# Attention and routed experts on one core: reads by 64 tokens, another order of the loads and of the routing steps

## The reference

```python
q_prime = relu(q @ Wqf.T); k_prime = relu(k @ Wkf.T) * mask      # q, k, v: projections, per head
kv = k_prime.T @ v;  k_sum = sum(k_prime)
att = (q_prime @ kv) / (q_prime @ k_sum + 1e-8)
x = x + att @ Wo.T + bo
p = softmax(layernorm(x) @ gate_w);  w, e = top_2(p);  w = w / sum(w)
x = x + sum_k w_k * ((silu(xn @ w1[e_k]) * (xn @ w3[e_k])) @ w2[e_k])   # xn = layernorm(x)
```

## Time and profile before

| | us |
|---|---|
| median of three runs | 497.66 |
| lowest, highest | 497.05, 499.25 |
| the profiled execution's own time | 499.79 |
| its span, first to last instruction | 497.9 |
| first expert product | 163.34 |
| first product of tile 4 | 209.09 |
| last output | 481.51 |

### The profile page before, as it was taken

The page is one execution under the profiler, slowest core; times in us unless marked ns, Lnnn a source line. Parts: engine busy times, 40 slices in busy tenths (PEclk is TensorE's granted clock), DMA queues, the critical chain, the costliest instruction groups (busy, mean ns, idle before and its releaser), DMA issues.

```text
span 497.9 us, 11763 instructions
## 1 busy us (share of the span) xinstructions
PE 447.2 (90%) x3665; PEld 416.3 (84%) x3666; DVE 208.6 (42%) x569; ACT 228.1 (46%) x477; POOL 231.6 (47%) x222
## 2 busy tenths in 40 slices
PE   3873999999989899799898999999999999999960
PEld 3773999889978788699898999899999999999960
DVE  4413766785485666623232323143323232332310
ACT  3614776647756255235542364263355264323210
POOL 5302638575858436119681249158139348121211
PEclk9995999999989899889999999999999999999985
DMA  8461101137102823381736212713621212121210
GB/s 257 142 224 41 44 24 65 65 103 231 63 22 76 286 44 101 89 268 33 243 80 200 44 32 34 244 32 92 194 32 33 32 32 30 34 32 32 35 23 11
DMA packets 34519, 46.05 MB, mean 92 GB/s; under 512 B 3488, under 2 KB 29344, under 8 KB 34464
## 3 DMA queue, kind: packets, MB, share of 16 engines
q1 hardware_dynamic: 22304, 31.82, 19.1%
q0 software_dynamic: 6576, 8.82, 10.3%
q10 hardware_dynamic: 5584, 4.76, 3.6%
HBM read 32.63 MB, written 12.76 MB: 91 GB/s over the span
## 4 chain that ended last, share of the span: by engine, by line
PE 66%; DMA 10%; DVE 8%; issue 5%; POOL 4%; ACT 3%; POOLq 1%; ACTq 0%; SPq 0%; DVEq 0%
PE bank L803 26%; PE twin L821 14%; DMA out_rows<-qf,x_all 6%; PE twin L674 5%; PE bank L840 3%; POOL w_lo L489 3%; DVE prob L1208 3%; PE bank L591 3%; PE bank L545 2%; PE bank L572 2%; DMA raw<-in_ctxT 2%; PE twin L665 2%; PE bank L546 2%; PE bank L608 2%; PE bank L547 2%
## 5 line engine op out<-in xcount | busy, mean ns | idle before, releaser
L499 POOL DMA_INDIRECT out_rows<-qf,x_all x35 | 54.6, 1560 | 158.9 <-ACT qf L1033 156.6
L803 PE MATMUL bank<-w_hi,c_hi 128*128 (+1 forms) x280 | 107.6, 384 | 4.1 <-POOL w_lo L489 1.6
L803 PE MATMUL bank<-w_lo,c_hi 128*128 (+1 forms) x280 | 104.1, 372 | 0.0
L821 PE MATMUL twin<-w_hi,kv_halves 128*128 (+1 forms) x490 | 97.2, 290 | 5.5 <-issue 5.0
L1292 DVE TENSOR_TENSOR x_all<-bank,x_all 128x448 f32<-128x448 f32 x70 | 43.4, 623 | 112.8 <-ACT x_all L1050 112.7
L821 PEld LDWEIGHTS twin<-w_hi,kv_halves 128*128 128x128 f32 x490 | 79.2, 192 | 6.4 <-issue 6.4
L1050 ACT ACTIVATE x_all<-bank 128x448 f32<-128x448 f32 x70 | 37.8, 544 | 96.3 <-PE bank L803 90.8
L489 POOL TENSOR_TENSOR w_lo<-raw,w_hi x18 | 76.2, 4436 | 10.0 <-ACT w_hi L1043 7.5
L803 PE MATMUL bank<-w_hi,c_lo 128*128 (+1 forms) x280 | 80.6, 370 | 0.0
L1298 DVE TENSOR_TENSOR kv_halves<-bank,kv_halves 128x512 fp32r<-128x512 f32 x66 | 38.6, 624 | 80.9 <-ACT kv_halves L1055 80.7
L821 PE MATMUL twin<-w_lo,kv_halves 128*128 (+1 forms) x245 | 69.7, 285 | 0.0
(11 more groups left out here) (218 smaller groups left out, 730.8 us busy)
## 6 DMA issues: line engine op xcount, KB each, us to landing
raw<-in_w SPq DMA_DIRECT2D x24, 896.0 KB, 7.5
x_all<-bucket ACTq DMA_DIRECT2D x31, 129.0 KB, 2.1
raw<-in_ctxT SPq DMA_DIRECT2D x8, 256.0 KB, 3.2
out_rows<-x_all SPq DMA_DIRECT2D x8, 256.0 KB, 2.1
bucket<-pad_rows SPq DMA_DIRECT2D x13, 129.0 KB, 3.3
x_all<-in_x SPq DMA_DIRECT2D x2, 512.0 KB, 6.5
x_all<-bucket SPq DMA_DIRECT2D x6, 129.0 KB, 2.7
x_all<-in_x SPq DMA_DIRECT2D x1, 768.0 KB, 6.6
```

Of the source, the lines that this page charges most:

```text
L499: pool.indirect_dma_start(out=out, out_offset=bass.IndirectOffsetOnAxis(ap=x_in[:, v, D:D + 1].bitcast(U32), axis=0), in_=y[:, v, :], in_o ...
L803: last = nc.tensor.matmul(bank[b][:, 0:MC], stationary[:, k, :], w[:, bass.ds(at + (of + k * M + c * MC), MC)], start=(k == 0 and part == ...
L821: last = nc.tensor.matmul(bank[6][:, 0:D], stationary[:, k, :], w[:, bass.ds(at + (2 * W13 + k * D), D)], start=(k == 0 and part == 0 and ...
```

## The change

- TensorE's `read` handles 64 tokens at a time, on array columns 0 to 63 and 64 to 127 in turn.
- SyncE loads the contexts of pairs 2 and 3 ahead of expert 0, which it loads in pass 2 of its loop. Later it writes all eight pads first, loads tile 4 from a constant row, then tile 5.
- VectorE makes the low keys (in round 7: the residual of pair 6) ahead of `best_two`. `split_x(1)`, `choices` of the last pair, the first list steps and `split_x(4)` move up in the hand-written part.
- TensorE and ScalarE take the transposes of tiles 1 and 4 earlier. GpSimd starts the last scatter ahead of an add. The number of tiles is read before the loops, and the last output takes a constant place of its weights.

```diff
...
             sp.dma_start(bucket[PAD_AT:PAD_AT + P, :], pad_rows[:]).then_inc(pad_stored[1], 16)
-            sp.wait_ge(wk_halves, 2)
-            sp.wait_ge(bdk_halves, 2)
-            sp.wait_ge(wv_halves, 2)
-            sp.wait_ge(bdq_halves, 2)
-            sp.wait_ge(wo_halves, 2)
-            load_expert(0)
             for i in range(NPR):
+                if i == 2:
+                    sp.wait_ge(wk_halves, 2)
+                    sp.wait_ge(bdk_halves, 2)
+                    sp.wait_ge(wv_halves, 2)
+                    sp.wait_ge(bdq_halves, 2)
+                    sp.wait_ge(wo_halves, 2)
+                    load_expert(0)
                 if i >= 2:
...
                 sp.dma_start(bucket[bass.ds(n + e * CAP, P), :], pad_rows[:]).then_inc(pad_stored[min(e, 2)], 16)
-            def load_first(t):
-                at = sp.value_load(tab_row[0:1, t:t + 1], min_val=0, max_val=PAD_AT)
-                sp.wait_ge(y_added, 16 * (t - 3))
-                sp.dma_start(x_in[:, t % 4, :], bucket[bass.ds(at, P), :]).then_inc(x_in_loaded[t % 4], 16)
             sp.wait_ge(list_ready, 1)
-            pad(0)
-            pad(1)
+            for e in range(E):
+                pad(e)
             for odd in range(2):
                 sp.wait_ge(scattered[odd], 32 * NPR)
+            sp.wait_ge(pad_stored[0], 16)
+            sp.wait_ge(y_added, 16)
+            sp.dma_start(x_in[:, 0, :], bucket[2 * P:3 * P, :]).then_inc(x_in_loaded[0], 16)
+            sp.wait_ge(pad_stored[1], 16 * 2)
             sp.wait_ge(list_ready, 3)
-            sp.wait_ge(pad_stored[0], 16)
-            load_first(AHEAD)
-            for e in range(2, E):
-                pad(e)
-            sp.wait_ge(pad_stored[1], 16 * 2)
-            load_first(AHEAD + 1)
+            at = sp.value_load(tab_row[0:1, AHEAD + 1:AHEAD + 2], min_val=0, max_val=PAD_AT)
+            sp.wait_ge(y_added, 16 * 2)
+            sp.dma_start(x_in[:, 1, :], bucket[bass.ds(at, P), :]).then_inc(x_in_loaded[1], 16)
             sp.wait_ge(logits_done, NPR)
...
             scatter(NPR - 2)
+            scatter(NPR - 1)
             add(1, 1)
-            scatter(NPR - 1)
             add(2, 2)
...
                 for j in range(PAIRS):
-                    last = nc.tensor.matmul(bank[6 + o][:, j * 2 * AUG:(j + 1) * 2 * AUG], qf[:, j, o * P:(o + 1) * P],
-                                            kv[:, o, j, :], start=True, stop=True)
+                    for half in range(2):
+                        at = o * P + half * (P // 2)
+                        last = nc.tensor.matmul(bank[6 + o][half * (P // 2):(half + 1) * (P // 2), j * 2 * AUG:(j + 1) * 2 * AUG],
+                                                qf[:, j, at:at + P // 2], kv[:, o, j, :], start=True, stop=True)
                 if o == 1:
...
                 last.then_inc(h_done, 1)
-            def output(t):
-                _, at = slot_at(t)
+            def output(t, at=None):
+                if at is None:
+                    _, at = slot_at(t)
                 if tile_live(t, -1):
...
             read(NPR - 1, 1)
+            x_transposes(1, 1)
             hidden(0, 1)
             transpose_x2(NPR - 2)
-            x_transposes(1, 1)
             transpose_attention(NPR - 1)
...
             hidden(3, 1)
+            x_transposes(4, 0)
             g_transposes(3)
...
             pe.wait_ge(list_ready, 7)
-            x_transposes(4, 0)
+            n = tiles_used(pe)
             tiles_of_mixture(pe, mix)
-            output(tiles_used(pe) - 1)
+            output(n - 1, (E - 1) % 2 * WALL)
         @block.scalar
...
                 at = act.value_load(tab_row[0:1, bass.ds(t, 1)], min_val=0, max_val=PAD_AT)
+                if isinstance(t, int) and t == AHEAD + 2:
+                    act.wait_ge(pad_stored[2], 16 * (E - 2))
                 if tile_live(t, -4):
...
                 act.wait_ge(xT_done, t + 1)
+                if isinstance(t, int) and t == 1:
+                    act.wait_ge(h_done, 2)
                 nc.scalar.copy(x_hi.rearrange("p k n -> p (k n)"), rows_bank(t)[:, 0:D]).then_inc(x_hi_ready, 1)
...
             silus(0, 0)
+            evacuate_x(1)
             silus(0, 1)
...
             high_attention(NPR - 1)
-            evacuate_x(1)
             exponents(NPR - 2)
...
             silus(3, 1)
+            evacuate_x(4)
             high_g(3)
-            evacuate_x(4)
-            act.wait_ge(pad_stored[2], 16 * (E - 2))
             act.wait_ge(list_ready, 7)
...
                 low_attention(i - 1)
+                if i + 1 < NPR:
+                    low_channels(kT_lo, kT_hi, bank[4], bk_s, kT_ready, kT_lo_ready, i + 1)
+                else:
+                    residual(i - 1)
                 if i >= 2:
                     best_two(i - 2)
-                if i + 1 < NPR:
-                    low_channels(kT_lo, kT_hi, bank[4], bk_s, kT_ready, kT_lo_ready, i + 1)
-                if i >= 2:
                     choices(i - 2)
...
             split_x(0)
-            residual(NPR - 2)
             rank_slots(NPR - 3)
...
             attend(NPR - 1)
+            split_x(1)
             gates(0, 1)
             low_attention(NPR - 1)
-            split_x(1)
             maxima(NPR - 2)
...
             best_two(NPR - 1)
+            choices(NPR - 1)
             gates(2, 0)
-            choices(NPR - 1)
             dve.wait_ge(list_step, 1)
...
             nc.vector.tensor_copy(tab_count[:], n_row[:]).then_inc(list_ready, 1)
-            gates(2, 1)
-            split_x(3)
             link(nc.vector.tensor_tensor(more, n_row[:].rearrange("a (e o) -> a e o", o=1).to_broadcast([1, E, NT]),
...
             link(nc.vector.tensor_scalar(ends[:, 0, :], n_tiles[:], 1.0, None, ALU.max))
-            low_g(2)
             for i, by in enumerate((1, 2, 4)):
...
                 link(nc.vector.tensor_tensor(ends[:, i + 1, by:E], ends[:, i, by:E], ends[:, i, 0:E - by], ALU.add))
+            gates(2, 1)
+            split_x(3)
+            low_g(2)
             link(nc.vector.tensor_tensor(past, tile_no[:].rearrange("a (t o) -> a t o", o=1).to_broadcast([1, TILES, E]), wide(ends[:, 3, :]), ALU.is_ge))
...
             gates(3, 1)
+            split_x(4)
             link(nc.vector.memset(lists[:, 4, 0:AHEAD + 1], 0.0))
...
             low_g(3)
-            split_x(4)
             dve.wait_ge(list_ready, 7)
...
```

## The result

| | before | after |
|---|---|---|
| runs shown, us | 497.38 (497.05 to 499.25, 4 runs) | 481.63 (480.38 to 483.93, 4 runs) |
| profiled execution, us (span) | 499.79 (497.9) | 480.38 (478.6) |

The ratio is 0.9681, 95% interval 0.9632 to 0.973. The direction was forecast, the size was not: 473.3, with a range up to 480.5.

A forecast was written before the change was run, and what follows sets the result against it. TensorE, working in 447.2 of 497.9 us, was taken as the bound. Terms 12.1 + 5.8 + 3.7 + 1.2 + 1.6 = 24.4 off the profiled 499.79 give 475.4, or 473.3 for the median; range 467 to 480.5.

The forecast's parts named there:

- Part 1: Contexts loaded before expert 0: TensorE's 10.2 us wait and the slow clock after it go, 12.1 us net.
- rival of the moved wait: Expert 0's transfer ends at 45, not 40.5; ScalarE then TensorE stand 2.5 to 4 us in round 2: 477, chance 0.12.
- the attention, 0.7: Next wait in pair 1's round: VectorE needs 1.37 us to the scaled attention, TensorE has 0.91 of work; about 0.7 us.
- Part 2: Reads on 64 columns take 1.05 us instead of 1.81; 5.8 us saved where TensorE sets the pace.
- rivals of 1.8 and 3.6 us: Read times: halves' weight loads take turns, 1.8 (479, chance 0.12); each record costs as before, 3.6 (503, chance 0.03).
- reads gain nothing: The two halves' weight loads take turns, so a read stays at 1.8 us: 479, chance 0.12.
- Part 3: Low keys ahead of `best_two`: TensorE's waits for them go; 3.7 us in rounds 4 to 7, reads included.
- routing does not hold: `prob` slips in before GpSimd's pieces; rounds 4 to 7 run at 15.5, 9 us more gained: 464, chance 0.12.
- The residual: Residual of pair 6 ahead of `prob`: the first expert product no longer waits for it; saves 0.8 us.
- Part 4: Early expert tiles: tile 1's transposes and tile 4's load come earlier, net of new waits; 1.2 us.
- the 0.8 less at tile 4: First product of tile 4, hanging on the last list and two register loads, comes at 208.3, 0.8 us earlier.
- Part 5: Tail: two of five register loads in TensorE's 4.10 us idle before the last output go; 1.6 us.

The follow-up runs named there:

- e15: The changed kernel with all reads back on 128 columns, on the fourth chip: 486.55 us, 0.9731 of the kernel before.
- e18: The changed kernel itself, unaltered, run again on the fourth chip: 481.2 us, 0.9626 of the kernel before.
- e3_keys_late: The changed kernel with low keys and the residual of pair 6 behind `best_two` again: 484.83 us, 0.965 of the kernel before.
- e14_changed_third: The changed kernel itself, unaltered, profiled again on the third chip: 490.75 us, 0.9834 of the kernel before.
- e12_fill: The changed kernel with the four second transposes done twice, ahead of the query features: 489.3 us, 0.9806 of the kernel before.

## Why the prediction was right and wrong

**Part 1 (12.1) held.** The wait is gone, ScalarE took the context at 26.75, and expert 0 arrived in time, so the rival of the moved wait fell. Round 2's values came 13.0 us earlier; with the two reads of the round I had 13.6. The new wait was not the one I named (the attention, 0.7) but 0.95 us before the transposes of x, whose normalising GpSimd holds, and 0.47 before the query features.

**Part 2 (5.8): the record was right, its worth was not.** 32 records take 1.06 us, forecast 1.05, so the rivals of 1.8 and 3.6 us fell. By e15 and e18 the first rank is 1.55 us earlier with short reads at equal clock (60.38, 58.83), where I had 3.0 for rounds 1 and 2. Up to `rank(1)` I had 17.15 and got 14.5. The step that failed is that TensorE sets the pace of rounds 1, 2 and 3, so that each keeps all of its 1.5 us: rounds 1 and 2 now have the two waits of part 1, and 0.65 us before the second transposes for low halves of the queries behind a held normalising, and from `rank(0)` on the wait for the low context takes 0.68. From there to `rank(4)` short reads are worth nothing. The rival "reads gain nothing" had 479 and comes nearer to 481.63 than the forecast, but by luck: a read did fall to 1.06. The Trainium skill (TensorE: Matmul & The Clock Gate, "The mechanism") has a weight load overlap a matmul only if the row group differs; the trace disagrees, as it did for the gathers: 0.033 us a record.

**Part 3 (3.7) failed by its main term.** From `rank(1)` to `rank(3)` 0.1 us was saved, not 1.9; from `rank(3)` to `rank(5)` 0.7, not 1.0. I had routing hold one round in two, at 17.4 us, and TensorE the other at 15.5 and 0.6. That is the step that failed: the rounds last 17.6 to 18.3, and no round falls to TensorE's own 15.9. Over the four rounds to `rank(4)` e15 and e18 are equally long, though TensorE has 1.1 to 1.5 us more to do in each of e15's. I take it that a round behind a held one is held too, since its `slots`, low context and `chosen` all come from the same two engines. It was my rival "routing does not hold" turned round; I gave a chance to the side on which it holds less and none to that on which it holds more. The keys themselves were right: no wait for low keys is left, and e3_keys_late has 2.8 us of it again. The residual saved 0.7 for 0.8. `prob` outlasted more than one piece once more (3.80 us, from within the second to the end of the third): the trace still disagrees with the Trainium skill's SBUF, State Buffer, "SBUF: two separate sides", by which the port pair is held for one instruction.

**Part 4 (1.2) failed at tile 4.** The early tiles gave 1.15 us (41.0 to 39.86 from tile 0 to the end of tile 3's hidden product), which with the last read's 0.75 is what I had. But the 0.8 less at tile 4 became 1.25 more. A pad took 8.90 / 8 = 1.11 us and not 0.97, the load was out at 186.41, 0.9 us before the end of tile 3's product, and behind the 1.70 us wait come the split, the last list and the register loads, 2.94 us of issue where I had 1.2. With two pads 4.6 to 5.1 us are enough, as before the change (4.76).

**Part 5 (1.6) held:** TensorE idles 2.25 us and not 4.10, and the shorter idle kept the upper clock: the last output takes 2.7 us, not 4.86. That brought little, as ScalarE is in its own tests until 467.1 and evacuates then: last output to the end is 15.9 for 16.4.

**The sum.** 24.4 less 4.85 in the rounds, 2.0 at tile 4, and 1.8 more than forecast behind it (0.25 in the tail's idle, 1.0 in the expert tiles, 0.5 at the end) is 19.3, the profiled gain. The other 3.6 us up to the medians are how two executions lay in their spread; I had allowed for the 2.1 of the one before. I had treated that spread as noise around a fixed clock; the mean clock of the four executions after goes from 0.976 to 0.964.

## What to carry to other kernels

A wait that is removed from the busiest engine is only worth what the next loop leaves: work out the period of every loop through the other engines, and if one is longer than the shortened round, it paces all rounds, not every second one. Before making an instruction of the bound engine cheaper, look for the short two-input VectorE operation that stands beside GpSimd's long ones and is on the way to the busy engine's next input; taking it out, with two pads for eight, gave 7.9 us beside reads of 128 columns (486.55 to 478.63), where the new read gave 5.4 on the same chip. And measure a small gain on more than one chip, with both kernels in each comparison.

## What was unexpected of the hardware

- **The clock can fall behind small waits.** A round with a few idle stretches of 0.2 to 0.9 us can end in some 3 to 7 us at the lower level (1.2 GHz): in e14_changed_third 0.16 and 0.57 us idle at 120.8 and 122.2, then 0.50 at 123 to 125. The changed kernel's first result had 1.6 us idle a round in one or two pieces, and no fall until the last, while e15_reads_128_again, after 0.83 us idle before 130.18, ran its next 22.89 us at 0.68. The time goes with the mean: over the 22 executions of the changed kernel on record a straight line falls by 4.6 us for each 0.01, and they lie up to 3.2 us off it (480.4 at 0.976, 482.7 at 0.971, 487.8 at 0.960, 493.9 at 0.948). What exactly brings a fall about wasn't found.
- **The same kernel differs between chips beyond its spread:** 481.6 in the first result, 488.5 and 490.75 on the third chip, 481.2 us on the fourth, while the kernel before took 498.6 to 498.9 beside the last three. The stall behind the second read, 0.9 to 1.6 us in five rounds with late word to VectorE and ScalarE, is the difference in the traces, with the falls of the clock that come with it. Its cause is open; that it moved with the work in its place (e12_fill) speaks against the query features as such.
- **VectorE is held beside GpSimd, once over more than one operation:** `prob`, 0.17 us alone, took 3.80 to the end of GpSimd's third piece. The two normalisings of 2.64 and 3.02 us are two operations each, of 1.3 to 1.5 us instead of 0.4 to 0.5, and each ended within 0.3 us of one GpSimd operation.
